# Up projections of a mixture of experts with the weights as the stationary operand, and the weights read from memory for each tile of tokens

## The reference, cut to what matters

```
x = x + gnn(layernorm(x), adj)            # 4 heads, masked softmax over 128 x 128
h = layernorm(x); z = h + attention(rmsnorm(h, ln1))
flat = rmsnorm(z, ln2)
w    = top2(softmax(flat @ router.T)), normalised
for e in range(8):
    hh  = silu(flat @ w1[e].T) * (flat @ w3[e].T)      # [tokens, 341] each
    out = out + w[:, e] * (hh @ w2[e].T)
return x + z + out
```

## Time and profile before

| what | value |
|---|---|
| median of 3 runs (lowest, highest) | 1985.65 us (1980.44, 1990.24) |
| the profiled execution: time, its span | 1984.17 us, 1982.4 us |
| granted TensorE clock, mean over the span | 0.956 of full speed |
| TensorE busy, weight loads busy | 1698.9 us (86%), 1308.2 us (66%) |
| VectorE busy | 1450.5 us (73%) |
| ScalarE busy | 926.4 us (47%) |
| GpSimd busy | 958.7 us (48%) |
| chain that ended last | PE 54%, DVE 20%, issue 8%, POOL 4%, ACT 4%, DMA 1% |
| DMA | 79.26 MB, mean 40 GB/s |
| q0 (issued by POOL), q1 (by SP): share of the 16 engines | 12.2%, 8.4% |

### The profile page before, as it was taken

The page is one execution under the profiler, slowest core; times in us unless marked ns, Lnnn a source line. Parts: engine busy times, 40 slices in busy tenths (PEclk is TensorE's granted clock), DMA queues, the critical chain, the costliest instruction groups (busy, mean ns, idle before and its releaser), DMA issues.

```text
span 1982.4 us, 39651 instructions
## 1 busy us (share of the span) xinstructions
PE 1698.9 (86%) x10546; PEld 1308.2 (66%) x10546; DVE 1450.5 (73%) x5051; ACT 926.4 (47%) x2779; POOL 958.7 (48%) x852
## 2 busy tenths in 40 slices
PE   3667777999999999999999999999999999988675
PEld 2545566777777777777777777777777777766343
DVE  3556666878888788788887888888888888865532
ACT  1344433555555554555554555445555555543121
POOL 1143466554445555555544555545555444554433
PEclk9888888999999999999999999999999999988897
DMA  4000111222222212222222222122222222212221
GB/s 121 7 26 20 37 33 37 43 40 41 43 41 43 43 34 37 45 43 42 42 42 41 41 44 43 31 41 44 44 40 43 42 44 40 38 34 40 38 32 18
DMA packets 142416, 79.26 MB, mean 40 GB/s; under 512 B 33048, under 2 KB 137564, under 8 KB 141949
## 3 DMA queue, kind: packets, MB, share of 16 engines
q0 software_dynamic: 47232, 34.92, 12.2%
q1 hardware_dynamic: 94973, 41.80, 8.4%
HBM read 33.39 MB, written 44.86 MB: 39 GB/s over the span
## 4 chain that ended last, share of the span: by engine, by line
PE 54%; DVE 20%; issue 8%; POOL 4%; ACT 4%; DMA 1%; DVEq 0%; POOLq 0%; SPq 0%; ACTq 0%
PE bank L1056 7%; PE bank L1075 6%; PE bank L967 5%; PE bank L1060 5%; PE bank L893 5%; PE bank L1068 4%; PE bank L980 4%; PE bank L1002 3%; PE bank L1009 2%; DVE z L638 2%; PE bank L929 2%; DVE hg L858 2%; POOL routed L398 2%; DVE fx L660 2%; PE bank L1019 1%
## 5 line engine op out<-in xcount | busy, mean ns | idle before, releaser
L419 POOL DMA_INDIRECT out<-ys,xt x264 | 426.3, 1615 | 519.3 <-DMA out<-ys,xt 252.6
L398 POOL DMA_INDIRECT routed<-fx,slot x256 | 256.2, 1001 | 141.5 <-DVE slot L779 77.5
L503 ACT ACTIVATE p<-ub,nm 128x128 f32<-128x128 f32 x512 | 163.6, 390 | 277.4 <-DVE nm L712 277.4
L1075 PE MATMUL bank<-w_s,hsT 128*128 (+1 forms) x1584 | 232.1, 283 | 27.8 <-ACT hsT L545 20.4
L858 DVE SCALAR_TENSOR_TENSOR hg<-sg,bank 128x341 f32<-128x341 f32 x264 | 134.7, 510 | 163.2 <-ACT sg L538 161.8
L1075 PEld LDWEIGHTS bank<-w_s,hsT 128*128 128x128 f32 (+1 forms) x1584 | 205.2, 193 | 68.5 <-issue 61.4
L1056 PE MATMUL bank<-w_s,xT 128*128 x528 | 218.4, 496 | 19.6 <-DVE xT L852 7.7
L1060 PE MATMUL bank<-w_s,xT 128*128 x528 | 202.7, 466 | 4.0 <-DVE hu L866 0.4
L511 ACT ACTIVATE p<-bank,nm 128x128 f32<-128x128 f32 x512 | 145.5, 365 | 118.1 <-DVE nm L718 118.0
L544 ACT ACTIVATE hsT<-bank 128x256 f32<-128x256 f32 x264 | 101.1, 383 | 154.0 <-PE bank L1068 152.8
L1068 PE MATMUL bank<-ident,hu 128*128 128x128 f32 (+1 forms) x792 | 136.3, 282 | 33.1 <-DVE hu L866 15.7
(11 more groups left out here) (172 smaller groups left out, 3484.4 us busy)
## 6 DMA issues: line engine op xcount, KB each, us to landing
xt<-routed SPq DMA_DIRECT2D x264, 65.0 KB, 1.8
xs<-in_x SPq DMA_DIRECT2D x32, 256.0 KB, 3.1
out<-bs SPq DMA_DIRECT2D x32, 256.0 KB, 2.3
out<-ys,xt POOLq DMA_INDIRECT x264, 3.4
routed<-fx,slot POOLq DMA_INDIRECT x256
w_s<-in_w SPq DMA_DIRECT2D x2, 1364.0 KB
adj<-in_adj SPq DMA_DIRECT2D x32, 64.0 KB, 3.3
w_s<-in_w SPq DMA_DIRECT2D x2, 512.0 KB
```

What stands on the lines that cost most here:

```text
L398: pool.indirect_dma_start(routed, bass.IndirectOffsetOnAxis(slot[p][:, i:i + 1], 0), fx[i // GB][p][:, i % GB, :], None).then_inc(S[f"sc{p ...
L419: pool.indirect_dma_start(out_rows, bass.IndirectOffsetOnAxis(xt[r][:, C:C + 1].bitcast(I32), 0), ys[r][:], None, compute_op=ALU.add).then ...
L503: last = act.activation(p1[j % 2][:, h, :], ub[j % 2][:, h, :], ACT.Exp, bias=nm1[:, j, h:h + 1])
L1075: last = pe.matmul(y_p[:, 0:C], hsT[r % 2][0:n, c, :], w2_s[0:n, bass.ds(e, 1), c, :].rearrange("p a c -> p (a c)"), start=c == 0, stop=c ...
```

## The change

The up projections swap their operands. For each tile the expert's `w1` and `w3` (one array in memory, each padded with zeros from 341 to 384 columns) are loaded by SP into one of three buffers `w13`, 128 x 768 numbers, 393216 bytes. Step `u` then holds a piece of 128 columns of the weights stationary and moves `xT` past it: three products of 128 columns for `w1` and three for `w3`, whose results have the hidden units on the partitions and the tokens along the free axis. That is the form that the down projection needs, so step `t` is gone on TensorE and ScalarE, and `hsT` with it. A new step `w` on SP reads the expert's number, waits until the third tile before has finished with the buffer (semaphore h3) and issues the load. The factor `ln2` is now multiplied in as VectorE copies `xT`, so the scaling of the weights by ScalarE is gone, and the factor 0.5 moves to `ys`. The list `ORDER` is another one, for all engines.

```diff
-ORDER = """T.yT G.xn A.hN E.l.0 E.l.1 E.x.0 G.h E.u.0 E.g.0 ...
+ORDER = """E.l.0 E.w.0 E.x.0 T.yT G.xn G.h A.hN E.u.0 E.g.0 T.wo E.x.1 ...
...
+                def load_weights(r):
+                    w = g - 4
+                    k = w * RING + r
...
+                    e = sp.value_load(expert_at(w, p, r), min_val=0, max_val=NE - 1)
+                    if k >= WB:
+                        sp.wait_ge(S["h3"], k - WB + 1)
+                    sp.dma_start(w13[k % WB][:].rearrange("c a n -> c (a n)"),
+                                 w13_h[bass.ds(e, 1)].rearrange("e c n -> c (e n)")).then_inc(S[f"wq{k % WB}"], 16)
...
-                    dve.tensor_copy(xT[r % 2][:], x_p[:, 0:128]).then_inc(S["xT"], 1)
+                    dve.tensor_scalar(xT[r % 2][:], x_p[:, 0:128], ln2c[:], None, ALU.mult).then_inc(S["xT"], 1)
...
                 def up(r):
-                    e = expert(r)
-                    pe.wait_ge(S["xT"], k8 + r + 1)
-                    pe.matmul(h1_p[:, 0:HID], xT[q][:], w1_s[:, bass.ds(e, 1), :].rearrange("c a n -> c (a n)"),
-                              start=True, stop=True).then_inc(S["h1"], 1)
-                    if late(k8, 1) or r:
-                        pe.wait_ge(S["hu"], k8 + r)
-                    pe.matmul(h3_p[:, 0:HID], xT[q][:], w3_s[:, bass.ds(e, 1), :].rearrange("c a n -> c (a n)"),
-                              start=True, stop=True).then_inc(S["h3"], 1)
-
-                def turn_h(r):
-                    for c, (o, n) in enumerate(HC):
-                        last = pe.transpose(hs_p[0:n, c * 128:(c + 1) * 128], hu[r % 2][:, o:o + n], ident[:])
+                    pe.wait_ge(S[f"wq{k % WB}"], 16 * (k // WB + 1))
+                    pe.wait_ge(S["xT"], k + 1)
+                    for c in range(3):
+                        last = pe.matmul(h1_p[:, c * 128:(c + 1) * 128], b[:, 0, c * 128:(c + 1) * 128], xT[r % 2][:], start=True, stop=True)
+                    last.then_inc(S["h1"], 1)
+                    if k:
+                        pe.wait_ge(S["hu"], k)
+                    for c in range(3):
+                        last = pe.matmul(h3_p[:, c * 128:(c + 1) * 128], b[:, 1, c * 128:(c + 1) * 128], xT[r % 2][:], start=True, stop=True)
+                    last.then_inc(S["h3"], 1)
```

More of the change, by code:

```diff
@@ L34 @@
 SKEW = HD - 1
+HP = 384
+WB = 3
 HC = [(0, 128), (128, 128), (256, HID - 256)]
@@ L90, in gnn_moe_block @@
 def gnn_moe_block(nc, x, adj, W, WT, att_src, att_dst, ln1, ln2, wq, wqr, wk, wkr, wv, wo, router,
-                  w1, w3, w2, rope_h, ident_h, causal_h, before_h, small_h, queue_h, out):
+                  w13_h, w2, rope_h, ident_h, causal_h, before_h, small_h, queue_h, out):
     ctx = ExitStack()
@@ L134, in gnn_moe_block @@
         rout = sb("rout", [C, 128])
-        w1_s = sb("w1_s", [C, NE, HID])
-        w3_s = sb("w3_s", [C, NE, HID])
+        w13 = [sb(f"w13_{i}", [C, 2, HP]) for i in range(WB)]
         w2_s = sb("w2_s", [128, NE, 3, C])
@@ L205, in gnn_moe_block @@
         rank_ps base bst0 bst1 sc0 sc1 pad padsc tabw table
-        last xtr xT h1 h3 htr sg hg hu hsT yp ys
+        last xtr xT h1 h3 sg hg hu yp ys
         zs turn_dve turn_pool turn_pe turn_sp""".split()
-        names += [f"{n}{r}" for n in ("xq",) for r in range(RING)]
+        names += [f"{n}{r}" for n in ("xq",) for r in range(RING)] + [f"wq{r}" for r in range(WB)]
         TABLE = 14
@@ L326, in load_tile @@
                     sp.dma_start(xt[r][:], src).then_inc(S[f"xq{r}"], 16)
-                return {"nx": nx, "f": f, "l": load_tile}
+                def load_weights(r):
+                    w = g - 4
+                    k = w * RING + r
+                    if r == 0:
+                        if is_last(w):
+                            sp.wait_ge(S["last"], 1)
+                        else:
+                            sp.wait_ge(S["table"], w + 1)
+                        sp.sem_inc(S["turn_sp"], 1)
+                    e = sp.value_load(expert_at(w, p, r), min_val=0, max_val=NE - 1)
[3 more added lines that the diff above has]
+                                 w13_h[bass.ds(e, 1)].rearrange("e c n -> c (e n)")).then_inc(S[f"wq{k % WB}"], 16)
+                return {"nx": nx, "f": f, "l": load_tile, "w": load_weights}
             phase1(sp, steps)
@@ L524, in out2 @@
                     act.activation(pT2[j % 2][:].rearrange("c b l -> c (b l)"), a1[:], ACT.Copy).then_inc(S["pT2"], 1)
-                def rank():
-                    if isinstance(g, int) and g == 2:
-                        act.wait_ge(S["ld_w"], 16 * 5)
-                        act.activation(w1_s[:], w1_s[:], ACT.Copy, scale=ln2c[:]).then_inc(S["wscale"], 1)
-                        act.activation(w3_s[:], w3_s[:], ACT.Copy, scale=ln2h[:]).then_inc(S["wscale"], 1)
                 k8 = (g - 4) * RING
@@ L857, in gate @@
                         dve.wait_ge(S["hu"], k8 + r - 1)
-                    dve.scalar_tensor_tensor(out=hg[r % 2][:], in0=sg[r % 2][:], scalar=1.0, in1=h1_p[:, 0:HID],
+                    dve.scalar_tensor_tensor(out=hg[r % 2][:], in0=sg[r % 2][:], scalar=1.0, in1=h1_p[:, 0:HP],
                                              op0=ALU.add, op1=ALU.mult).then_inc(S["hg"], 1)
@@ L1038, in turn_x @@
                 def turn_x(r):
-                    if isinstance(g, int) and g == 4 and r == 0:
-                        pe.wait_ge(S["wscale"], 2)
                     pe.wait_ge(S[f"xq{r}"], 2 * k8 + 16)
@@ L1046, in up, with down @@
                 def up(r):
-                    q = r % 2
+                    k = k8 + r
+                    b = w13[k % WB]
+                    pe.wait_ge(S[f"wq{k % WB}"], 16 * (k // WB + 1))
[8 more added lines that the diff above has]
+                    last.then_inc(S["h3"], 1)
+                def down(r):
                     if r == 0:
@@ L1098, in turned, with wide @@
         return np.concatenate([w[:, HD // 2:], w[:, :HD // 2]], 1)
+    def wide(w):
+        return np.pad(w.transpose(0, 2, 1), ((0, 0), (0, 0), (0, HP - HID)))
     def cols(w):
@@ L1107 @@
         "wk": cols(wkh), "wkr": cols(turned(wkh)), "wv": cols(wvh), "wo": a["ffn_wo"].T, "router": a["ffn_router_w"].T,
-        "w1": a["ffn_w1"].transpose(2, 0, 1), "w3": a["ffn_w3"].transpose(2, 0, 1), "w2": a["ffn_w2"].transpose(0, 2, 1),
+        "w13_h": np.concatenate([wide(a["ffn_w1"]), wide(a["ffn_w3"])], 2), "w2": a["ffn_w2"].transpose(0, 2, 1),
         "rope_h": tb["rope"], "ident_h": tb["ident"], "causal_h": tb["causal"], "before_h": tb["before"],
```

50 lines of the change are left out of this document (20 added, 30 removed).

## The result

| | runs | median us | lowest to highest |
|---|---|---|---|
| before | 4 | 1985.01 | 1980.44 to 1990.24 |
| after | 4 | 2259.19 | 2249.17 to 2266.64 |

The ratio is 1.1377, with a 95% interval of 1.1324 to 1.1430: the change makes the kernel 274 us slower. The forecast was 98 us slower, with a range that ended at 2135. So the sign was right and the size far too small.

What follows compares the result with a forecast made beforehand. No engine bounds it, but a loop through several with TensorE's work in the middle; 2.9 - 0.8 + 1.3 - 1.6 + 1.8 = 3.6 us per body, 101 in all, then +5 - 7: 1984.17 becomes 2083 us, range 1925 to 2135.

Steps and rivals of the forecast that it cites:

- `bs` ends: GpSimd's end of the residual bs, which SyncE's store waits for: 0.5 us earlier, bounds 3 earlier and 1 later.
- its landing: Tile 3's load arriving after its issue on SyncE: taken as 1.9 us, between bounds of 1.8 and 3.72.
- tile 3 to the rank: TensorE from tile 3's transpose to the rank, with tile 4's load behind w.6: 7.7 us against 8.48, so -0.8.
- rank to the statistics: Fourth residual sum behind the eighth scatter on GpSimd, +1.3 us; VectorE starting the statistics without its wait, -1.6.
- statistics to hN: VectorE does one more hg, hu, ys and xT behind the statistics before hN: +1.8 us.
- all of it outside the bodies: Two bodies without stage E +5 us; last three bodies -19 for TensorE and ScalarE copies, +12 for SyncE waits.
- the lower clock behind the wait: TensorE at 1.2 GHz after idling before tile 3: 0 to 1.5 us per body, up to 42, not summed.
- 3.72 for both landings: Upper bound for the landings of tiles 3 and 4: a body costs 3.8 us more, 2190 us in all.
- the up step: TensorE's up products: 1.33 us per tile, 0.15 less, and 0.29 per tile saved by no longer reading a register.
- the narrow products: 128-column passes on TensorE cost the same per column as 341-column ones within 5%; some 110 us dearer given no chance.
- loads hidden: Rival: tile 3 is there when TensorE is; +0.1 us per body, 1985 us (1965 to 2005), chance 0.16.
- The saving arrives: Rival: TensorE sets the pace, some 40% of its 116 us reach the end; 1938 us (1890 to 1976), chance 0.26.

Runs made afterwards that it cites:

- e9: The changed kernel with every weight load at its place and with its gates, but 48 KB instead of 384 KB each: ratio 1.0942, 2178.31 us.
- e3: The changed kernel with the steps in the order of the kernel before and the weight loads set into it: ratio 0.9995, 1994.42 us.
- e5: The changed kernel with, on SyncE alone, the loads of tiles 3, 4 and 5 right behind the store of the base rows: ratio 1.0427, 2081.64 us.
- e6: As e5, with hN's transposes and their copy ahead of the GNN projection again on TensorE and ScalarE: ratio 1.0453, 2085.30 us.
- e7: As e6, with the fourth residual sum on GpSimd ahead of the eighth routed scatter and tile 3's row scatter again: ratio 1.0217, 2039.60 us.
- e10: As e3, with SyncE's queue alone changed: weight loads 3 to 5 ahead of tile 3's load, load 6 ahead of tile 4's: ratio 1.1001, 2191.01 us.
- e1: The changed kernel without the weight loads, its tables staying on the chip and tile r always using expert r's: ratio 1.034, 2065.89 us.
- e2: As e1, with the steps of all engines in the order of the kernel before, less the dropped transposes: ratio 0.9974, 1989.55 us.

## Why the prediction was right in sign and wrong in size

| step of the loop | forecast | body at 1061.11 |
|---|---|---|
| `bs` ends | -0.5 | 14.97 for 14.76 into the body: +0.2 |
| issue of tile 3's load behind `bs` | 5.8 | 5.54 |
| its landing | 1.9 | 3.96 |
| tile 3 in all | +2.9 | 24.47 for 19.12: +5.35 |
| tile 3 to the rank | -0.8 | 9.61 for 8.48: +1.13 |
| rank to the statistics | 1.3 - 1.6 = -0.3 | 19.75 for 20.52: -0.77 |
| statistics to hN | +1.8 | 9.47 for 5.98: +3.49 |
| a body | +3.6 | +9.20 (mean of 28: +8.98) |
| all of it outside the bodies | 5 - 7 = -2 | +22 |

Three terms failed: the landing of tile 3's load (1.9 forecast, 3.96 measured), the lower clock behind the wait, which the sum left out, and TensorE's part of the step from the statistics to `hN`. Two slips of the adding are small: 5.8 + 1.9 is 7.7 and not 7.8, and with 3.72 for both landings a body costs 3.6 more and not 3.8.

**The step that failed first is the landing of tile 3's load.** The mechanism, its place, the pace of the queue and the engine that waits were as predicted: idle time ahead of tile 3, released by the load, of 3.53 us in a forecast of 2 to 4. I reckoned that 0.97 us are enough to move `w.5`, at the 404 GB/s of the earlier trace rows, and so gave the tile 1.9. What stood ahead of the tile was not one load but the store, three weight loads and the next inputs, together 1.8 MB issued within 4.5 us. They were moved like this (columns as in the earlier trace rows):

```profile
1077.00:1085.50 8.50, 4.37 (x30) 3.32 (x29) 5.05 (x11) 5.43 (x15) 2.45 (x2) 1.00 0.86 233
```

233 GB/s with the DMA engines 86% busy. By an estimate from the two rates, 1.8 MB take 4.4 us at 404 GB/s, no longer than their issue, and no backlog forms; at 233 they take 7.6. I had taken a rate from a stretch of wide rows and applied it to a mix with rows of 128 and 512 bytes, and I had counted the average load of a body (7.8 of 55 us) where the queue's backlog at one moment decides. e9 shows the term by itself: an eighth of the weights' bytes, and the landing is 1.78. It also shows that this term is less than half of the miss. With the landing as short as forecast the kernel still takes 2178 us, 95 more than the 2083, and its mean wait for tiles 3 and 4 between 450 and 1700 is 2.1 us a body (41.0 in 20). The upper bound was in the text (3.72 for both landings, 2190 us), but the range ended at 2135, below it.

The Trainium skill says (DMA: Bandwidth & Descriptors, Why small descriptors are slow) that each packet carries a fixed overhead of about 3 cycles, so that rows of some hundred bytes move slower. The 233 against 404 GB/s agree with it in direction only: 3 cycles on the 16 of a 512-byte row are about a sixth, an estimate from that page, and the fall is larger. No run here took the small rows away, so why the rate was 233 stays open. The rule of the Trainium skill on order within a ring (same page, Queues, rings and completion order), used in the prediction, fits: tile 3 lands as the backlog ends, and the DMA engines' share falls from 0.86 to 0.02 at 1085, as the row below shows. But the price worked out from the page there, 1.8 us for the landing, came from the same full rate, and failed with it.

**Tile 3 to the rank** was priced at full clock: 3.3 us to the end of h3. It took 4.70 (1085.58 to 1090.28), since the clock fell behind the idle time:

```profile
1085.00:1087.00 2.00, 1.42 (x10) 1.42 (x11) 0.35 (x1) 0.00 (x0) 0.00 (x0) 0.86 0.02 3
1087.00:1089.00 2.00, 2.00 (x12) 2.00 (x11) 1.59 (x16) 0.19 (x1) 0.00 (x0) 0.50 0.00 0
```

I had named the low clock, with 0 to 1.5 us a body, and left it out of the sum. It was far more: against e3, with the same work for TensorE, the changed kernel's engine is busy 52.5 us of a body instead of 48.4, and 130 us longer in all. Tile 4's load then landed late too, 2.4 us after its issue.

**Statistics to hN.** VectorE's part came out as forecast, 1122.68 - 1114.94 = 7.74 for 7.78, but partly by luck: it holds a wait of 0.80 us for TensorE's down product of tile 7, which I had not counted.

```profile
1119.00 0.35 DVE L876 TENSOR_SCALAR ys<-bank,xt 128x128 f32<-128x128 f32 x1 [0.80 <-PE bank L1072]
```

I had priced `hg`, `hu` and `ys` behind the statistics as VectorE's work alone. But TensorE's down product of tile 7 waits for the `ys` of tile 6, 1.42 us in this body and 3.03 in e5, and VectorE's next `ys` then waits for that product. TensorE's 1.73 us behind VectorE were missed as well. They are not the projection's place (e6), so what they cost by themselves is not settled; they stand on the same engine at the same low clock. After all three places are put back (e7), 56.8 us a body remain against 54.6. At the opening of a body of e7 and of e3:

```profile
1027.27 1.97 PE L929 MATMUL bank<-wh,xnT 128*128 128x132 f32 x8
1029.03 1.49 PE L1050 MATMUL bank<-xT,w 128*128 128x128 f32 x6
1030.31 1.40 PE L1055 MATMUL bank<-xT,w 128*128 128x128 f32 x6
```

```profile
946.05 1.07 PE L929 MATMUL bank<-wh,xnT 128*128 128x132 f32 x8
946.95 0.83 PE L1050 MATMUL bank<-xT,w 128*128 128x128 f32 x6
947.62 0.83 PE L1055 MATMUL bank<-xT,w 128*128 128x128 f32 x6
```

From the first start to the end of the third these pieces take 2.0 us longer in e7, near the 2.2 that remain. But the wait of 1.2 us for tile 0 in e7 is of that order too, and so are the 1.5 us a body by which all of TensorE's work is longer (1674.7 us busy for 1633.9). Which of them it is, is not shown: e7 and e3 differ in the order of every engine, and e10 warns that full clock at the opening does not make a body short.

**Outside the bodies.** I had the last three bodies 7 us shorter on balance. Without loads (e1) the part behind the last opening is indeed 15 us shorter (205.0 for 220.3), near the 19 that I reckoned for TensorE's and ScalarE's copies; with loads it is 20 longer. The 12 us that I put against it for SyncE should have been 35 (240.2 - 205.0). That the reason is the one of the bodies is likely, but not shown.

**What held:** the up step (0.67 + 0.67 us at full clock, forecast 1.33), the 46 and 63 ns on VectorE (549 and 345 ns measured, forecast 556 and 345), the narrow products, and no gain from TensorE's shorter work. The up step's waits on issue did not go with the register: its weight loads (L1050) waited 46.6 us on issue between 400 and 1700 in the changed kernel and 88.7 in e3, against the 54.0 of the earlier trace rows. So the 0.29 us a tile that I had put down to the register is not shown by those waits.

The rival "loads hidden" had tile 3 in time in the new order and +0.1 us a body, 1985 us in all. e5 is that case, and its bodies are 58.0 us long, 3.4 more than before. So the steps at the end of the body were priced too low even with tile 3 out of the account. That e3 comes near the 1985 us, with 1994, is chance, since it has none of those steps. "The saving arrives" is refuted by e2 and e3, where the loads are absent or hidden and TensorE does less, and the time stays.

## What to carry to other kernels

The landing of a load depended on the bytes that stood ahead of it in its queue at that moment (3.96 us, and 1.78 with an eighth of the weights' bytes), and on the rate at which that mix moved; the mean share of bandwidth in the loop said nothing about it. A new wait on an engine costs more than its length, if its clock is lower behind it: price the work that follows at the lower clock as well. When a change adds bulk loads to a queue that also carries small loads on the critical path, put each small load ahead of every bulk load that need not be earlier: here that one edit was worth 158 us with one load moved, and in the old order the bulk traffic itself cost nothing that could be told. When a change comes with a new order, undo the order alone first: here it took back all of the 14% in one run, and the single moves behind it showed that a wait that is plainly to be seen (the projection ahead of hN) need not be a cost. When an instruction that waits for another engine is moved ahead in its queue, look at what the other engines need from behind it, as TensorE needed `ys` from behind the statistics.
